# An attention and FFN kernel on one core: down projection made transposed, one more FFN product on GpSimd, and fillers on TensorE between the stages

## The reference

```
scale_x = sigmoid(clip_x) * max|x| / 127           # one maximum over ALL tokens
xq   = clip(round(x / scale_x), -128, 127) * scale_x
gate = xq @ quantised(w_gate).T                    # 128 -> 352
up   = xq @ quantised(w_up).T                      # 128 -> 352
h    = silu(gate) * up
scale_h = sigmoid(clip_down) * max|h| / 127        # again one maximum over ALL of h
hq   = clip(round(h / scale_h), -128, 127) * scale_h
out  = hq @ quantised(w_down).T                    # 352 -> 128, each row of w_down with its own scale
result = x_in + out
```

## Time and profile before

| | |
|---|---|
| three runs | 282.92 us median (282.5 to 284.82) |
| the profiled execution | 284.12 us, of which the profile's span is 282.3 us |
| mean granted TensorE clock | 0.975 of full speed |
| PE busy | 258.2 us, 91% of the span |
| DVE busy | 234.2 us, 83% |
| ACT busy | 225.4 us, 80% |
| POOL busy | 201.4 us, 71% |
| moved by DMA | 6.48 MB |

### The profile page before, as it was taken

The page is one execution under the profiler, slowest core; times in us unless marked ns, Lnnn a source line. Parts: engine busy times, 40 slices in busy tenths (PEclk is TensorE's granted clock), DMA queues, the critical chain, the costliest instruction groups (busy, mean ns, idle before and its releaser), DMA issues.

```text
span 282.3 us, 7419 instructions
## 1 busy us (share of the span) xinstructions
PE 258.2 (91%) x2210; PEld 209.5 (74%) x2210; DVE 234.2 (83%) x973; ACT 225.4 (80%) x778; POOL 201.4 (71%) x395
## 2 busy tenths in 40 slices
PE   6789899999999999999999999999999999988171
PEld 5457678888888888888888888888888877752060
DVE  5799797898889888988898889787977779879893
ACT  2587888988889898999899989998899898258380
POOL 6385878988798879888987888878878885013310
PEclk9999999999999999999999999999999999999757
DMA  5648000000000000000000000000000200000014
GB/s 136 182 117 188 1 2 1 2 3 0 3 0 5 0 3 0 2 1 3 0 2 3 2 0 2 1 3 2 0 2 2 78 2 1 2 4 2 1 34 119
DMA packets 12110, 6.48 MB, mean 23 GB/s; under 512 B 1615, under 2 KB 11940, under 8 KB 12069
## 3 DMA queue, kind: packets, MB, share of 16 engines
q1 hardware_dynamic: 11642, 5.78, 7.7%
q10 hardware_dynamic: 426, 0.20, 0.2%
HBM read 4.88 MB, written 1.07 MB: 21 GB/s over the span
## 4 chain that ended last, share of the span: by engine, by line
PE 79%; DVE 10%; ACT 4%; issue 3%; POOL 1%; DMA 1%; DVEq 0%; ACTq 0%; POOLq 0%
PE bank L976 16%; PE bank L927 11%; PE front L953 9%; PE back L1019 7%; PE front L1019 7%; PE bank L790 7%; PE back L953 6%; PE bank L808 5%; DVE score L1376 2%; ACT bias L749 2%; PE front L766 1%; PE bank L934 1%; ACT prob L744 1%; DVE prob L1543 1%; PE bank L906 1%
## 5 line engine op out<-in xcount | busy, mean ns | idle before, releaser
L633 ACT ACTIVATE prob<-score,negmax 128x258 f32<-128x258 f32 (+1 forms) x256 | 113.7, 451 | 17.5 <-DVE negmax L1376 17.4
L491 POOL TENSOR_SCALAR prob<-prob,rrow 128x258 f32<-128x258 f32 x254 | 105.8, 436 | 19.4 <-DVE rrow L1384 16.0
L450 POOL TENSOR_TENSOR rq<-qn,neghalf 128x8 f32<-128x8 f32 x32 | 53.7, 1679 | 2.7
L633 ACT ACTIVATION_READ_ACCUMULATOR prob<-score,negmax 128x1 f32 x256 | 49.3, 192 | 0.0
L976 PE MATMUL bank<-pT,val 128*64 128x256 f32 x496 | 47.9, 335 | 0.0
L976 PEld LDWEIGHTS bank<-pT,val 128*64 128x64 f32 x496 | 30.3, 136 | 15.2 <-issue 4.9
L1376 DVE CUSTOM_DVE_ANT_0 score<-front,bias 128x258 f32<-128x258 f32 (+1 forms) x128 | 38.0, 354 | 2.0 <-PE front L953 1.8
L1376 DVE CUSTOM_DVE_ANT_0 score<-back,bias 128x258 f32<-128x258 f32 (+1 forms) x128 | 37.4, 349 | 0.0
L927 PE MATMUL bank<-wout,oT 128*128 128x128 f32 x256 | 36.8, 288 | 0.4 <-DVE oT L1366 0.4
L1366 DVE COPY oT<-bank 128x512 f32<-128x512 f32 x32 | 22.1, 689 | 16.1 <-PE bank L976 15.9
L927 PEld LDWEIGHTS bank<-wout,oT 128*128 128x128 f32 x256 | 30.9, 191 | 4.4 <-DVE oT L1366 0.8
(11 more groups left out here) (228 smaller groups left out, 469.9 us busy)
## 6 DMA issues: line engine op xcount, KB each, us to landing
bias<-relative_table SPq DMA_DIRECT2D x8, 256.0 KB, 5.1
X<-in_x_dram SPq DMA_DIRECT2D x1, 896.0 KB, 5.4
out_dram<-prob SPq DMA_DIRECT2D x3, 256.0 KB, 2.5
prob<-in_L_cond_Wq_dram SPq DMA_DIRECT2D x1, 512.0 KB, 3.8
wout<-in_L_cond_Wout_dram SPq DMA_DIRECT2D x1, 512.0 KB, 5.3
prob<-in_L_ffn_w_down_dram SPq DMA_DIRECT2D x1, 176.0 KB, 2.4
X<-in_x_dram SPq DMA_DIRECT2D x1, 128.0 KB, 2.1
prob<-in_L_ffn_w_gate_dram SPq DMA_DIRECT2D x1, 128.0 KB, 2.2
```

The lines of the kernel that those rows point to most:

```text
L450: pool.tensor_tensor(dst, src, neghalf[:, 0:width], ALU.pow).then_inc(done, 1)
L491: pool.tensor_scalar(prob[:, par, h, cols], prob[:, par, h, cols], rrow[:, par, h, t:t + 1], 1.0, ALU.mult, ALU.mult).then_inc(normed, 1)
L633: act.activation(prob[:, par, h, cols], score[:, h % 4, cols], ACT.Exp, scale=-1.0, bias=negmax[:, par, h, t:t + 1], accum_out=rowsum[:, p ...
```

## The change: what it does

- `POOLED` gets a fifth tile, (2, 1); the buffers between ScalarE and GpSimd become three, and lie in the `bias` tile, which nobody reads any more.
- The casts of x: chunks 0, 3 and 1 by VectorE, chunk 2 by GpSimd; ScalarE has none.
- The order of VectorE's products and maxima in the gate and up stage is written out, with the maxima of the third tiles later.
- TensorE gets fillers: five behind each of the maxima number 6 to 10, eleven behind the spread of the maximum, three behind each of the first two quantised tiles.
- The casts of h: eight by ScalarE, those of (2, 2) and (3, 0) by VectorE behind all eleven quantises, that of (3, 1) by GpSimd.
- Down, chunk 0 as before (tokens on the partitions), tile by tile. Chunks 1, 2 and 3 are made transposed: weights stationary, 512 tokens streaming, features on the partitions. There the scale is one value per partition (`sdc`), which ScalarE applies as it copies PSUM to SBUF (`down_evac`; chunk 3 in two halves), TensorE turns the copy back in blocks of 128 (`down_turn`), and VectorE adds x straight out of PSUM (`residual`).
- Chunk 0's addition of x is GpSimd's. Stores: chunk 1, 0, 2, then the two halves of chunk 3, all issued by SP.

The diff, without the declarations of semaphores:

```diff
--- before.py
+++ after.py
@@ -42,8 +42,11 @@
 LAST = 3
 TILES = [(k, f) for k in range(4) for f in range(IT) if (k, f) != (LAST, IT - 1)]
 ORDER = {tile: n for n, tile in enumerate(TILES)}
-POOLED = [(0, IT - 1), (1, IT - 1), (2, IT - 1), (LAST, 0)]
+POOLED = [(0, IT - 1), (1, IT - 1), (2, 1), (2, IT - 1), (LAST, 0)]
 MADE = [tile for tile in TILES if tile not in POOLED]
+CAST_POOL = [(LAST, 1)]
+CAST_DVE = [(2, IT - 1), (LAST, 0)]
+CAST_ACT = [tile for tile in TILES if tile not in CAST_POOL and tile not in CAST_DVE]
 
 
 def scale_of(k, f):
...
@@ -252,9 +255,11 @@
         res = spare[:, IT * B * N:(IT + 1) * B * N].rearrange("p (t c) -> p t c", c=C)
         hmax = sb("hmax", [P, len(TILES)])
 
-        last_gate, last_up = (spare[:, IT * B * N + 1024 * a:IT * B * N + 1024 * (a + 1)]
-                              .rearrange("p (a n) -> p a n", a=2) for a in range(2))
+        last_gate, last_up = (bias[:, :, :].rearrange("p h n -> p (h n)")[:, 1536 * a:1536 * (a + 1)]
+                              .rearrange("p (a n) -> p a n", a=3) for a in range(2))
         sds = sb("sds", [P, C])
+        sdc = sb("sdc", [P, 1])
+        downT = hT[:, 0, :].rearrange("p (k n) -> p k n", k=4)
 
 
         def psum(name, banks):
...
@@ -283,8 +288,9 @@
 
             return misc[:, t * P:t * P + P]
 
-        gate_ps, up_ps, down_ps = bank[0:3], bank[3:6], bank[6:8]
-        last_down_ps = bank[2:6]
+        gate_ps, up_ps = bank[0:3], bank[3:6]
+        down_ps = [bank[i] for i in (6, 7, 0, 1)]
+        turned_ps = bank[2:6]
         q_ps0 = [bank[i] for i in (5, 2, 4, 5)]
         hid_ps = bank[1][:, 0:N].rearrange("p (t c) -> p t c", t=2)
         gcols_ps, keys_ps = qT_ps[:, 0:P], qT_ps[:, P:P + 2 * D + H]
...
@@ -414,11 +421,12 @@
             sp.wait_ge(wdp_zero, 1)
             for k in range(LAST):
                 sp.dma_start(wdp[IL:P, k, :], wT[IR * k:IR * k + IR, 2, IT - 1, :]).then_inc(ld_down, 16)
-            for k in range(3):
+            for k in (1, 0, 2):
                 sp.wait_ge(res_ready[k], 1)
                 sp.dma_start(out_dram[:, 4 * k:4 * k + 4, :], res[:, 4 * k:4 * k + 4, :]).then_inc(stored, 16)
-            sp.wait_ge(res_last, 1)
-            sp.dma_start(out_dram[:, 12:14, :], res[:, 12:14, :]).then_inc(stored, 16)
+            for half, t0 in enumerate((4 * LAST, 4 * LAST + 2)):
+                sp.wait_ge(res_last, half + 1)
+                sp.dma_start(out_dram[:, t0:t0 + 2, :], res[:, t0:t0 + 2, :]).then_inc(stored, 16)
             sp.wait_ge(stored, 16 * 5)
 
 
...
@@ -526,12 +534,21 @@
             pool.wait_ge(ld_scale, 16 * LAST)
             pool.tensor_scalar(sgu[:, :, :], wsp[:, :, :], asc[:, 0:1], 1.0, ALU.mult, ALU.mult).then_inc(sgu_ready, 1)
 
+            def x_cast(k, done):
+
+                pool.wait_ge(x8, done)
+                pool.tensor_copy(xqb[:, 512 * k:512 * k + 512], xq[:, 512 * k:512 * k + 512]).then_inc(xq_pool, 1)
+
+            x_cast(2, 4)
             for n, (k, f) in enumerate(POOLED):
                 pool.wait_ge(last_ready, 2 * (n + 1))
-                pool.tensor_tensor(hT[:, f, 512 * k:512 * k + 512], last_gate[:, n % 2, :], last_up[:, n % 2, :],
+                pool.tensor_tensor(hT[:, f, 512 * k:512 * k + 512], last_gate[:, n % 3, :], last_up[:, n % 3, :],
                                    ALU.mult).then_inc(last_done, 1)
-            pool.wait_ge(scaled, 2)
-            pool.tensor_tensor(res[:, 4:8, :], res[:, 4:8, :], X[:, 4:8, :], ALU.add).then_inc(res_ready[1], 1)
+            for k, f in CAST_POOL:
+                pool.wait_ge(h8, ORDER[k, f] + 1)
+                pool.tensor_copy(hqb[:, f, 512 * k:512 * k + 512], hq[:, f, 512 * k:512 * k + 512]).then_inc(hq_pool, 1)
+            pool.wait_ge(scaled, 1)
+            pool.tensor_tensor(res[:, 0:4, :], res[:, 0:4, :], X[:, 0:4, :], ALU.add).then_inc(res_ready[0], 1)
 
 
         @block.scalar
...
@@ -717,12 +734,6 @@
 
 
             act.activation(table_load[:, 2:3], neghalf[:, 0:1], ACT.Silu)
-            def x_cast(k, done):
...
-            x_cast(LAST, 2)
             act.wait_ge(sgu_ready, 1)
             for k, f in TILES:
                 act.wait_ge(gu_done, ORDER[k, f] + 1)
...
@@ -735,20 +746,31 @@
                                    scale=sgu[:, at, 0:1]).then_inc(gate_ready, 1)
                 else:
                     n = POOLED.index((k, f))
-                    if n > 1:
...
-                    act.activation(last_gate[:, n % 2, :], gate_ps[f][:, :], ACT.Silu,
+                    if n > 2:
+                        act.wait_ge(last_done, n - 2)
+                    act.activation(last_gate[:, n % 3, :], gate_ps[f][:, :], ACT.Silu,
                                    scale=sgu[:, at, 0:1]).then_inc(last_ready, 1)
-                    act.activation(last_up[:, n % 2, :], up_ps[f][:, :], ACT.Copy,
+                    act.activation(last_up[:, n % 3, :], up_ps[f][:, :], ACT.Copy,
                                    scale=sgu[:, at, 1:2]).then_inc(last_ready, 1)
 
-            for n, (k, f) in enumerate(TILES):
...
-            act.dma_start(out_dram[:, 14:16, :], res[:, 14:16, :]).then_inc(stored, 16)
+            def h_cast(k, f):
+
+                act.wait_ge(h8, ORDER[k, f] + 1)
+                act.copy(hqb[:, f, 512 * k:512 * k + 512], hq[:, f, 512 * k:512 * k + 512]).then_inc(hq_act, 1)
+
+            def down_evac(k, half):
+
+                act.wait_ge(down_done, k + 1)
+                act.wait_ge(sdc_ready, 1)
+                cols = slice(0, 512) if half is None else slice(256 * half, 256 * half + 256)
+                act.activation(downT[:, k, cols], down_ps[k][:, cols], ACT.Copy, scale=sdc[:, 0:1]).then_inc(downT_ready, 1)
+
+            for k, f in CAST_ACT:
+                h_cast(k, f)
+            for k in range(1, LAST):
+                down_evac(k, None)
+            for half in range(2):
+                down_evac(LAST, half)
 
 
         @block.tensor
...
@@ -1134,14 +1156,14 @@
                 keep_busy(12, q_ps)
                 pe.wait_ge(w_a, 4)
                 for k, f in TILES:
-                    if (k, f) in ((0, 0), (1, 0)):
...
-                        pe.wait_ge(last_ready, 2 * k)
+                    if (k, f) in ((0, 0), (0, IT - 1), (1, 0)):
+                        pe.wait_ge(xq_ready, ((0, 0), (0, IT - 1), (1, 0)).index((k, f)) + 1)
+                    if (k, f) == (2, 0):
+                        pe.wait_ge(xq_pool, 1)
+                    if k and (k - 1, f) in POOLED:
+                        pe.wait_ge(last_ready, 2 * (POOLED.index((k - 1, f)) + 1))
                     elif k:
-                        pe.wait_ge(h_ready, (k - 1) * (IT - 1) + f + 1)
+                        pe.wait_ge(h_ready, MADE.index((k - 1, f)) + 1)
                     packed = f == IT - 1
                     for a, ps in ((0, gate_ps[f]), (1, up_ps[f])):
                         last = pe.matmul(ps[:, :], wT[:, a, f, :], xqb[:, 512 * k:512 * k + 512], start=True,
...
@@ -1152,32 +1174,66 @@
                                              skip_group_check=True)
                     last.then_inc(gu_done, 1)
 
+                for n in range(len(TILES) - 5, len(TILES)):
+                    pe.wait_ge(hmax_ready, n)
+                    keep_busy(5, bank[6])
                 over_partitions(1)
-                for k in range(3):
-                    pe.wait_ge(hq_ready, IT * (k + 1))
-                    if k > 1:
-                        pe.wait_ge(scaled, k - 1)
+                keep_busy(11, bank[6])
+                for n in range(2):
+                    pe.wait_ge(h8, n + 1)
+                    keep_busy(3, bank[6])
+
+                def cast_done(k, f):
+
+                    if (k, f) in CAST_POOL:
+                        pe.wait_ge(hq_pool, CAST_POOL.index((k, f)) + 1)
+                    elif (k, f) in CAST_DVE:
+                        pe.wait_ge(hq_dve, CAST_DVE.index((k, f)) + 1)
+                    else:
+                        pe.wait_ge(hq_act, CAST_ACT.index((k, f)) + 1)
+
+                def down_make(k):
+
+                    for f in range(IT):
+                        cast_done(k, f)
+                        product = pe.matmul(down_ps[k][:, :], wT[:, 2, f, :], hqb[:, f, 512 * k:512 * k + 512],
+                                            start=f == 0, stop=f == IT - 1)
+                    product.then_inc(down_done, 1)
+
+                def down_turn(k, n, blocks):
+
+                    pe.wait_ge(downT_ready, n + 1)
+                    for j, blk in enumerate(blocks):
+                        product = pe.transpose(turned_ps[n][:, j * P:j * P + P], downT[:, k, blk * P:blk * P + P],
+                                               ident[:, :])
+                    product.then_inc(down_turned, 1)
+
+                def down_packed(k):
+
+                    pe.matmul(down_ps[LAST][:, :], wdp[:, k, :], hqb[:, IT - 1, 512 * k:512 * k + 512],
+                              start=k == 0, stop=False)
+
```

(107 more changed lines are left out.)

30 lines of the change are left out of this document (removed).

## The result

The changed kernel takes **282.40 us** (median of 20 runs, 282.26 to 282.79). The kernel before, now with 20 runs, takes 284.17 (282.39 to 284.82): the three runs shown first had given 282.92. The ratio of all runs is **0.9948**, 95% interval 0.9933 to 0.9963, so the kernel became faster by 0.5%, less than 1%; the two medians alone give 0.9938. The forecast was 281.1.

What follows compares the result with a forecast made beforehand. Bound: the tail behind 250 us, ScalarE's casts its largest piece, then store transfer. Gate and up (0.6), scale (0.18) and down stage issue the last store 2.3 us earlier; the store burst leaves 1.75, so 282.92 becomes 281.1, range 279.3 to 282.8.

Steps and rivals of the forecast that it cites:

- the one from the sum to the median: Whole kernel: the 1.75 us gain was taken off the median of 282.92, not the profiled 284.12, giving 281.1.
- one engine's tail: End of the stores: one of sixteen DMA engines drags on alone to about 281.5; without it 1.35 us less.
- Fillers: TensorE behind gate and up: fillers keep the full clock, shortening the maximum's spread by 0.18 us.
- Gate and up: Gate and up stage: VectorE's last maximum ends at 265.45 instead of 266.03, gain 0.6 us, bounds 0 and 1.2.
- The rival with nothing won ahead of Q: Gate and up: GpSimd's three products in a row slip and VectorE waits instead of working; 281.7 us, chance 0.10.
- Q: Moment of the first quantise, behind the scale: forecast to move from 267.59 to 266.82 us.
- Down stage: From the first quantise on: chunk 1's store issued at Q+6.96, the fifth at Q+8.85, 2.3 us earlier than before.
- The slower rival: Down stage: GpSimd's cast beyond 1.75 us delays chunk 0's addition and later stores; at 5 us 286.0, chance 0.05.
- Stores: End of kernel: five stores, 1 MB, transfer in one burst of 3.7 us from 274.7 to 278.4; gain 1.75 us.
- the 0.50 case: Whole kernel: the forecast itself, 281.1 us, own range 280.4 to 281.8, chance 0.50 of lying within 1%.
- the straggler's going (0.22): End of the stores: median runs pay the dragging engine's 1.35 us now, the changed kernel doesn't; 279.8 us, chance 0.22.
- Clock falls anyway (0.09): Scale and down stage: fillers fail to hold the full clock, costing 1.4 us together; 282.5 us, chance 0.09.

Runs made afterwards that it cites:

- the lower level: Faster of two groups of the kernel before's timed runs, unchanged: 13 of 31 took 281.95 to 282.65 us at a mean granted clock of 0.981 to 0.988.
- the upper level: Slower of two groups of the kernel before's timed runs, unchanged: 18 of 31 took 283.84 to 284.88 us at a mean granted clock of 0.974 to 0.976.
- the quantise above: Changed kernel with chunk 0 scaled by VectorE, added by GpSimd and stored early, chunk 1's transposes ahead of chunk 2's third product: 282.77 us.
- both ways of moving the jump: Two variants of the changed kernel: TensorE's FFN program behind the mask branch, 283.94 us; the branch's two arms exchanged, 287.5 us.

## Why the prediction was wrong, by its steps

**The step that failed is the one from the sum to the median.** The sum against the profiled run gave two figures: 282.4 with one engine's tail as it was, 281.0 without. The forecast then took the 1.75 off the median of three, 282.92, and read the 1.2 us between this and the profiled run as "most runs having no such tail, or paying it in both kernels". The first is refuted as far as traces go: the usual run of the old kernel takes 284.2 (the median of 20 is 284.17), and in all five of its traces the tail is there. The second came, for the new kernel keeps a tail of 0.8 us; but then the base had to be the profiled run, and the 282.4 worked out from it stands beside a measured 282.26. That two of the first three runs took 282.5 and 282.92 was the draw. Most likely the 282.5 was of the lower level, of which the mean clock is higher. For 282.92 it stays open: no clock is on record for it, it lies above the 13 lower runs, and runs at 282.83 and 283.0 had the upper level's clock. From the usual run to 282.4 it is 1.8 us, against 282.92 it is 0.5.

That 1.8 us is so near to the 1.75 of the sum is in part luck. The sixteen engines were through at 279.0, 0.6 us later than the forecast 278.4, and the tail behind them was 0.8 us instead of the 1.35 taken over from before. Two small slips stand in the sum as well: 282.92 - 1.75 is 281.17, and 0.22 with 0.07 makes 0.29 for faster, not 0.31.

**Fillers, mis-sized in the old kernel.** I gave the clock 0.18 us (the spread; 0.49 became 0.34) and hid the rest behind casts. In the new kernel the fillers are worth 0.9, in the old one 1.9 (284.17 to 282.27). Of the span's 2.1, 1.3 is work that ends earlier, since twelve products and what follows them stood in the chain of the earlier trace rows behind the last cast; the other 0.8 is the end without the tail. Everything was priced for the kernel as a whole, never for the fillers alone; that would have shown how much of the gain they can give.

**Gate and up: right in kind.** Last maximum at 265.67, forecast 265.45, before 266.03: 0.36 instead of 0.6. GpSimd's chain began 0.07 later than walked, and VectorE's waits for its own last products added the rest. The rival with nothing won ahead of Q is refuted: this part alone gives 0.57.

**Down stage: right.** First store at Q+6.96, as forecast, though that it agrees to the hundredth is chance. GpSimd's cast took 0.61 alone (0.72 taken), 1.07 beside VectorE's two, which kept their 0.75: GpSimd was the one to wait, off the path. The Trainium skill's rule ("SBUF — State Buffer", "Who interferes with whom": one of the two blocks fully) agrees with the quantise above that took 1.50 us beside an addition and 0.48 without. The slower rival, a cast of more than 1.75 us, is refuted.

**Stores: the mechanism right, two terms short.** The burst, begun by the first late store, takes 4.0 us instead of 3.7. The tail behind it adds 0.8; I had seen such a tail in the earlier trace rows and had taken it for something that may come or go. With both ways of moving the jump the fetch left the stores and 1.0 us went. So the 0.50 case had the right mechanism on the wrong base, and the straggler's going (0.22) did not happen.

**Clock falls anyway (0.09): refuted.** The granted clock stays at 1.00 with nothing but transposes on TensorE from 261.4 to 268.4; without the fillers it is at 0.50 in the window 264 to 266. The Trainium skill's "TensorE: Matmul & The Clock Gate", Part 4, would have had it fall; these runs, with f32 transposes of 128x128, go against it.

## What to carry to other kernels

Ask of every run shown which level it is of: where the times of one kernel split, compare the clocks, before a base is chosen, and price the cheapest part of a change (here 42 fillers) by itself, since the rest may be riding on it. Work that ends earlier can be worth nothing if its results leave in one burst: count the bytes behind the first late store, and what else uses the DMA engines then.

## What the runs showed of the hardware

- In one run of a kernel the half clock came 1.5 us into a gap in TensorE's work (266.56 to 268.0); in two of its ten runs there was hardly any half clock (0.993 and 0.994 on average).
- A jump of TensorE cost 1.8 us of delay at 248 us and 4.4 us of idle time at 20 us, and when it stood behind the last product, a 16 KB fetch of 0.93 us on one DMA engine in the midst of the stores. The fetches came in pairs, 3.1 to 4.2 us apart, and none ran there once the jump was moved.
- VectorE's quantise from SBUF to SBUF (0.48 us) took 1.50 beside a GpSimd addition with two inputs, which itself took 1.44 instead of 1.27; a GpSimd cast went from 0.61 to 1.07 beside VectorE's casts.
- The issue of a store grew from 0.41 to 1.35 us over five issued within 2.6 us on SP's queue, at no cost to the end here.
